# Softmax sums from columns of ones beside V, and scores in 64x64 tiles, in a cross-attention and expert kernel

## The chip, the cores and the metric

The kernel runs on one core of a Trainium2 chip. The metric is device time in microseconds (us) of one execution. A core has TensorE (PE, matmuls; its weight loads are listed as PEld), VectorE (DVE), ScalarE (ACT), GpSimd (POOL) and SyncE (SP, which here only issues DMAs). Each engine works through its own instruction list in order and waits on semaphores.

## The reference, cut to what matters

All data is float32. There are 64 batches of 64 query rows of 256 values, and 64 context rows of 128 values for each batch. The first part is a residual cross-attention with 16 heads of 16 values:

```
xn   = layernorm(x)                              # 64 x 64 x 256
q    = head_norm(xn @ Wq + bq)                   # per head of 16 values
main = the first 48 context rows, dca = the last 16
k, v = head_norm(main @ Wk..), main @ Wv..       # bk, bv beside
kd, vd from dca with their own weights
ctx  = softmax(q k^T / 4) v  +  softmax(q kd^T / 4) vd   # two softmaxes, 48 and 16 keys
x    = x + ctx @ Wo + bo
```

The second part is a residual feed-forward with a shared expert and 16 routed experts, two for each row. The change doesn't touch it, but for where some small buffers of its router lie.

## The kernel before, in words

The 64 batches are 32 pairs (128 query rows fill the 128 partitions), and two pairs (u = 0, 1) are one group, so there are 16 groups. The attention is a software pipeline over groups, written by hand: `main_loop` calls each engine's `step(i)` for i from -1 to 17, of which i = 3 to 12 is a hardware loop. In one step(i) each engine works on several groups: x of i+3 is loaded, x, q, k and v of i+2 are projected, q and k of i+1 are normalised and laid out, softmax and the product with V belong to i, the output projection and the residual to i-1, the second layer norm to i-2. The order of the calls in `step` is the order on that engine, and an instruction that waits holds up all behind it.

- VectorE: `inverse_roots` (L1361) makes all inverse square roots of a step in a chain of ten small instructions, the first of them L353; the maxima and subtractions of the scores of u = 0 stand between them. Then `residual` (L1460), `spread_roots` (L1421), `inverse_sums` of u = 0 (L1451: two sums and one reciprocal), maxima and subtractions of u = 1, `residual_stats`, `copy_qkv` (L1406), `inverse_sums` of u = 1, `x_stats`, `head_vars`. L1343 is the last instruction of either layer norm's statistics, on 128x2 values.
- GpSimd: `normalise_k` and `normalise_q` (L637, L646), which writes q twice, once for each batch of the pair, with zeros for the rows of the other batch; `normalise_probs` (L670), `add_bo` (L631), `dca_blocks` (L658).
- TensorE: `transpose_y`, `attn_out(i-1)` (L1098), `scores(i, 1)` (L1050), transposes of x, k and xn2, `project_q`, `transpose_q` of u = 0, `project_kv`, `transpose_q` of u = 1, `transpose_probs(i, 0)`, `route`, `probs_v(i, 0)` (L1077), `scores(i+1, 0)`, `transpose_probs(i, 1)`, `probs_v(i, 1)`.
- ScalarE: copies between PSUM and SBUF, exponentials, the two normalisations of x, squares, and `mask_v` (L800), which masks the V rows to block form.
- SyncE: `replicate_v` (L478) copies V rows and the stored DCA rows to both halves of the partitions (8 DMAs a step), then the loads of y and x and the stores of xn2.

Scores: one transposed q of 128 rows holds two heads' values and both batches by zeros; four matmuls of 128x128 by 256 columns fill `score_ps`. The probabilities are divided by their sums on GpSimd before they are transposed; `probs_v` multiplies with block V into a transposed context directly, which ScalarE copies for the output projection.

Of the kernel before, what the change touches and what calls it, by code (L numbers as in the profile page):

```python
# [25 lines left out]
P = 128  # L26
NB, SQ, D = 64, 64, 256
SK, KD = 64, 128
DCA = 16
# [12 lines left out]
CW = 4 * SK  # L42
HP = H // 2
TT = PAIRS // 2
SLOT_TILES = 48
N_CONST = 12
# [41 lines left out]
def xattn_moe(nc, x, ctx, Wq, bq, Wk, bk, Wv, bv, Wkvd, bkvd, qn_w, qn_b, kn_w, kn_b, kd_w, kd_b, Wo, bo,  # L88
              router, e_bias, w_up, w_down, sh_up, sh_down, out):
    stack = ExitStack()  # L90
    with stack:
# [3 lines left out]
        def sem(name):  # L95
            return stack.enter_context(nc.semaphore(name))

        bank = [stack.enter_context(nc.psum_tensor(f"bank{i}", [P, 512], F32)) for i in range(4, 8)]
# [3 lines left out]
               [b[:, :] for b in bank]  # L102


        vd_dram = nc.dram_tensor("vd_dram", [PAIRS * DCA, 2 * D], F32, kind="Internal").ap()
        vd_blocks = vd_dram.rearrange("(u t k) n -> t u k n", u=8, k=DCA)
# [9 lines left out]
        half = sb("half", [P, 2])  # L116
        slotm = sb("slotm", [P, 2])
# [6 lines left out]
        bkv_sb = sb("bkv_sb", [P, 2 * D])  # L124
# [7 lines left out]
        q_bias2 = sb("q_bias2", [P, 2])  # L132
# [13 lines left out]
        sel = sb("sel", [P, PAIRS, E])  # L146
        pair_sums = sb("pair_sums", [P, TT * NG, 6])
        gsum = sb("gsum", [P, TT, NG])
        gtmp = sb("gtmp", [P, TT, NG])
        goh = sb("goh", [P, 2, TT, NG])  # L150
        oh = sb("oh", [P, 2, PAIRS, E])
        etmp = sb("etmp", [P, PAIRS, E])
        tile_cnt = sb("tile_cnt", [P, PAIRS, E])
# [7 lines left out]
        past = sb("past", [1, SLOT_TILES, E])  # L161
# [5 lines left out]
        desc = sb("desc", [P, 1, E])  # L167

# [11 lines left out]
        kv_sb = sbl("kv_sb", [P, 2, 2 * D])  # L180
        sq = sbl("sq", [P, 2, 2, D])
        qn = sbl("qn", [P, 2, 2 * D])
# [4 lines left out]
        q_rstd2 = sbl("q_rstd2", [P, 2, H, 2])  # L187
        qT = sbl("qT", [P, 2, SETS, P])
        k_bd = sbl("k_bd", [P, 2, SETS, 4, SK])
        v_rep = sbl("v_rep", [P, 2, 2 * D])  # L190
        v_bd = sbl("v_bd", [P, 2, 2 * D])
        probs = sbl("probs", [P, 2, H, SK])
        pmax = sbl("pmax", [P, 2, 2, H])
        psum_ = sbl("psum_", [P, 2, 2, H])
        prec = sbl("prec", [P, 2, 2, H])
# [14 lines left out]
        kv_d = XN2[:, 0:4 * DT, :].rearrange("p (n c) d -> p n (c d)", c=2)  # L210
        sq_d = XN2[:, 4 * DT:6 * DT, :]
        kn_d = XN2[:, 6 * DT:8 * DT, :].rearrange("p (t c) d -> p t (c d)", c=2)
# [45 lines left out]
        s_sum = sem("softmax_sums")  # L258
# [11 lines left out]
        s_rstd = sem("head_rstd_ready")  # L270
# [7 lines left out]
        s_v = sem("v_replicated")  # L278
        s_vbd = sem("v_blocks_ready")
# [60 lines left out]

        x_rows = x.rearrange("b s d -> (b s) d")
        out_rows = out.rearrange("b s d -> (b s) d")

        def row1(v):
            return v.rearrange("(a n) -> a n", a=1)

# [1410 lines left out]
```

## Time and profile before

| | us |
|---|---|
| median of 3 runs | 643.29 |
| lowest to highest | 641.64 to 643.62 |
| span of the profiled execution | 644.6 |
| VectorE busy | 453.7 (70%) |
| TensorE busy | 525.5 (82%) |
| ScalarE busy | 348.8 (54%) |
| GpSimd busy | 288.1 (45%) |

The profile gives one execution's span, from its first to its last instruction, and no time around it. The attention takes from some 43 us to 383 us, the routing and the experts follow. Busy times overlap between engines; whoever wants to know what sets the time must ask which engine waits for which, in each stage.

### The profile page before, as it was taken

The page shows a single profiled execution, that of the slowest core. Times are in us where ns is not written, and L with a number is a line of the kernel's source. Part 1 is how long each engine was busy: PE and PEld are TensorE (multiplying, and loading weights), DVE is VectorE, ACT ScalarE, POOL GpSimd, SP SyncE. Part 2 cuts the span into 40 slices and gives each one's busy share as a digit, 9 for nine tenths or more (in the row PEclk, how much of TensorE's full clock was granted, in tenths as well). Part 3 has the DMA queues.
Part 4 walks back from the last instruction along what each step waited for, and adds up shares of the span by engine and source line. Part 5 has one row for each costly group of instructions (what it writes and reads, how often), then busy time and mean ns, then how long its engine had stood idle before and what let it go on. Part 6 is the DMA issues. An engine that isn't in the chain of part 4 may idle for free.

```text
span 644.6 us, 12343 instructions
## 1 busy us (share of the span) xinstructions
PE 525.5 (82%) x3539; PEld 410.0 (64%) x3540; DVE 453.7 (70%) x1114; ACT 348.8 (54%) x663; POOL 288.1 (45%) x358
## 2 busy tenths in 40 slices
PE   4457879878797788887898688994799998879977
PEld 2234657666575666766676555764799987865746
DVE  2966899999999998989987858985144446741343
ACT  1235668666786667857677426140566665506240
POOL 2012565534655346443465200577772057605760
PEclk9778998899999989979898879999699999879989
DMA  5251233243432434323333311953799788838343
GB/s 146 90 126 49 74 105 107 70 129 110 132 108 67 130 108 132 97 78 122 112 115 115 131 66 51 344 184 105 232 329 317 230 276 261 279 115 263 114 135 108
DMA packets 83052, 94.50 MB, mean 147 GB/s; under 512 B 8000, under 2 KB 72272, under 8 KB 83024
## 3 DMA queue, kind: packets, MB, share of 16 engines
q1 hardware_dynamic: 72976, 72.14, 36.0%
q0 software_dynamic: 6144, 16.79, 8.0%
q10 hardware_dynamic: 3904, 5.24, 2.7%
q8 instruction: 13, 0.21, 0.1%
q14 instruction: 15, 0.12, 0.1%
HBM read 40.66 MB, written 42.99 MB: 130 GB/s over the span
## 4 chain that ended last, share of the span: by engine, by line
PE 27%; POOL 24%; issue 22%; DVE 14%; DMA 4%; ACT 2%; DVEq 1%; POOLq 0%; ACTq 0%; SPq 0%
POOL slot_x L704 5%; PE bank L1276 4%; POOL probs L673 4%; POOL kdT L721 4%; PE score_ps L1264 4%; POOL XN L721 3%; PE bank L1185 3%; POOL qn L652 3%; PE probsT_ps L1251 2%; PE probsT_ps L1103 2%; PE bank L1017 2%; PE score_ps L1026 2%; POOL k_bd L665 2%; POOL kn L641 2%; DVE psum_ L1454 2%
## 5 line engine op out<-in xcount | busy, mean ns | idle before, releaser
L673 POOL TENSOR_TENSOR probs<-probs,prec 128x768 f32<-128x768 f32 x64 | 65.7, 1046 | 53.6 <-DVE prec L1458 53.6
L704 POOL DMA_INDIRECT slot_x<-XN,slot_i x64 | 62.3, 973 | 55.4 <-DVE slot_i L1610 36.2
L641 POOL TENSOR_TENSOR kn<-kv_sb,rst 96x512 f32<-96x512 f32 x16 | 16.9, 1054 | 136.4 <-DVE q_rstd L1425 136.4
L1060 PE MATMUL score_ps<-k_bd,qT 128*128 128x256 f32 x256 | 66.9, 407 | 4.7 <-DVE probs L1446 3.6
L740 ACT ACTIVATE probsT<-probsT_ps 128x1024 f32<-128x1024 f32 x32 | 32.8, 1024 | 55.6 <-PE probsT_ps L1073 55.6
L1185 PE MATMUL bank<-sd_sb,hid 128*128 128x256 f32 x256 | 58.8, 392 | 3.5 <-DVE res L1728 3.5
L1060 PEld LDWEIGHTS score_ps<-k_bd,qT 128*128 128x128 f32 x256 | 50.7, 203 | 13.7 <-issue 5.2
L1185 PEld LDWEIGHTS bank<-sd_sb,hid 128*128 128x128 f32 x256 | 50.6, 198 | 12.5 <-issue 5.2
L1276 PE MATMUL bank<-down_sb,ea 128*128 x192 | 49.3, 404 | 8.2 <-DVE ea L1662 8.2
L1073 PE MATMUL probsT_ps<-ident,probs 128*128 128x128 f32 x256 | 35.3, 282 | 21.6 <-POOL probs L673 21.6
L1669 DVE COPY ey<-bank 128x512 f32<-128x512 f32 x48 | 30.9, 684 | 23.1 <-PE bank L1276 23.1
L1073 PEld LDWEIGHTS probsT_ps<-ident,probs 128*128 128x128 f32 x256 | 29.1, 144 | 28.2 <-POOL probs L673 27.9
L1092 PE MATMUL bank<-probsT,v_bd 128*32 128x64 f32 x1024 | 25.2, 243 | 26.6 <-ACT probsT L740 26.5
L1264 PEld LDWEIGHTS score_ps<-XN,tile_w 128*128 128x128 f32 x384 | 46.1, 197 | 0.8 <-issue 0.2
L1264 PE MATMUL score_ps<-XN,tile_w 128*128 128x128 f32 x384 | 46.3, 280 | 0.0
L1276 PEld LDWEIGHTS bank<-down_sb,ea 128*128 128x128 f32 x192 | 37.2, 204 | 13.6 <-issue 8.8
L1436 DVE TENSOR_REDUCE pmax<-score_ps 128x16 f32<-128x768 f32 x64 | 41.7, 672 | 5.1 <-PE score_ps L1060 5.0
L1446 DVE TENSOR_TENSOR probs<-score_ps,pmax 128x768 f32<-128x768 f32 x64 | 42.3, 682 | 0.0
L740 ACT ACTIVATE XN<-probsT_ps 128x512 f32<-128x512 f32 x48 | 26.0, 595 | 28.6 <-PE probsT_ps L1251 28.6
L1454 DVE TENSOR_REDUCE psum_<-probs 128x16 f32<-128x768 f32 x64 | 40.6, 673 | 0.5 <-ACT probs L812 0.3
L1092 PEld LDWEIGHTS bank<-probsT,v_bd 128*32 128x32 f32 x1024 | 20.3, 121 | 31.4 <-issue 31.3
L1103 PE MATMUL probsT_ps<-wo_sb,ctxT 128*128 128x256 f32 x128 | 40.0, 468 | 0.0
(210 smaller groups left out, 1210.9 us busy)
## 6 DMA issues: line engine op xcount, KB each, us to landing
slot_x<-zeros SPq DMA_DIRECT2D x32, 384.0 KB, 3.4
XN<-slot_x SPq DMA_DIRECT2D x24, 512.0 KB
slot_y<-ey SPq DMA_DIRECT2D x24, 512.0 KB, 3.9
v_rep<-kv_sb SPq DMA_DIRECT2D x64, 96.0 KB, 2.3
x_in<-in_x SPq DMA_DIRECT2D x16, 256.0 KB, 2.7
XN<-xn SPq DMA_DIRECT2D x16, 256.0 KB, 2.8
xn2T_dram<-xn2T SPq DMA_DIRECT2D x32, 128.0 KB, 2.3
xT_ch<-xn2T_dram SPq DMA_DIRECT2D x8, 512.0 KB, 4.8
```

Source lines behind the costliest of these rows:

```text
L673: last = pool.tensor_tensor(probs[:, u, :, lo:hi], probs[:, u, :, lo:hi], prec[:, u, c, :].unsqueeze(2).to_broadcast([P, H, hi - lo]), ALU ...
L704: pool.indirect_dma_start(slot_x[f][:, :], bass.IndirectOffsetOnAxis(ap=slot_i[:, k, t:t + 1], axis=0), XN2[:, t, :], None).then_inc(s_sca ...
L721: pool.indirect_dma_start(gath[b][:, h, k, j, :], None, slot_y[f][:, :], bass.IndirectOffsetOnAxis(ap=gidx[:, b, h, k, j:j + 1], axis=0))\
L740: return act.activation(dst, src, ACT.Copy)
L1060: last = pe.matmul(score_ps[:, s * CW:(s + 1) * CW], qT[:, u, s, :], k_bd[:, u, s, :, :].rearrange("p j k -> p (j k)"), start=True, stop=True)
L1073: last = pe.transpose(probsT_ps[:, n // 4, (n % 4) * P:(n % 4 + 1) * P], flat[:, n * P:(n + 1) * P], ident[:, :])
L1092: last = pe.matmul(ctx_ps[u][32 * n:32 * n + 32, col:col + 64], v_bd[:, u, b * D + (4 * c + n) * 32:b * D + (4 * c + n) * 32 + 32], probsT ...
L1103: last = pe.matmul(bank[2 + u][:, 0:D], ctxT[:, u, k, :], wo_sb[:, k, :], start=(k == 0), stop=(k == KC - 1))
L1185: last = pe.matmul(o, hid[:, j, m, t * P:(t + 1) * P], sd_sb[:, m, :], start=(m == 0), stop=(m == NM - 1))
L1264: last = pe.matmul(bank[h][:, j * P:(j + 1) * P], tile_w[:, h, j, k * MI:(k + 1) * MI], xtT[:, h, j, k, :], start=(k == 0), stop=(k == KC ...
L1276: last = pe.matmul(bank[4 + 2 * h + j // 2][:, (j % 2) * D:(j % 2 + 1) * D], ea[:, h, j * P:(j + 1) * P], down_w[:, bass.ds(offs[j], D)], ...
L1454: dve.tensor_reduce(psum_[:, u, c, :], probs[:, u, :, lo:hi], AX.X, ALU.add).then_inc(s_sum, 1)
```

## The change

- The product with V is turned round: the transposed probabilities are the stationary operand and V the moving one. For each pair of heads V stands in a row of 68 columns: 34 for the main keys (32 values, a 1, a 0), 34 for the DCA keys (with 0 and 1). So one product gives, for each head pair, the two softmaxes' unnormalised contexts and their sums. VectorE takes the reciprocals of the sums and multiplies the product (`normalise_ctx`), GpSimd adds the main and DCA parts (`add_ctx`), TensorE transposes the context (`transpose_ctx`), ScalarE copies it (`copy_ctx`), then comes the output projection, now after `transpose_q` and ahead of `project_kv`.
- The sums on VectorE and the products on GpSimd (`normalise_probs`) go, as does `spread_roots`.
- q is no longer doubled; the scores are eight matmuls of 64 rows by 64 columns of the array.
- V is written by VectorE with its padding, and SyncE places rows of 1088 values (`place_v`, double-buffered); ScalarE's `mask_v` goes.
- The residual of both pairs is one instruction and stands behind the subtractions of u = 1, ahead of `copy_qkv`.
- The hardware loop's body holds two steps.

```diff
+PVW = 2 * (2 * HD + 2)
+VROW = H // 2 * PVW
-            with eng.Fori(3, GROUPS - 3) as i:
-                step(i)
+            with eng.Fori(0, (GROUPS - 6) // 2) as m:
+                step(2 * m + 3, 1)
+                step(2 * m + 4, 0)
...
# setup: bias loads
-            sp.dma_start(bkv_sb[:, 0:D], all_rows(bk)).then_inc(s_w, 16)
-            sp.dma_start(bkv_sb[:, D:], all_rows(bv)).then_inc(s_w, 16)
+            for c, v in enumerate((bk, bv)):
+                key, value = (v.rearrange("(h t d) -> t h d", t=2, d=HD)[t] for t in range(2))
+                sp.dma_start(heads_of(bk_sb[:, :])[:, c * HP:(c + 1) * HP, :], all_rows(key)).then_inc(s_w, 16)
+                for b in range(2):
+                    sp.dma_start(heads_of(bv_sb[:, b, :])[:, c * HP:(c + 1) * HP, :], all_rows(value)).then_inc(s_w, 16)
...
# SyncE
+            def place_v(g, par):
                 wait_alone(sp, s_kv, g + 1)
-                if since(g, 1):
-                    sp.wait_ge(s_vbd, g)
-                for c in range(2):
+                if since(g, 2):
+                    sp.wait_ge(s_pv_ps, 2 * g - 2)
+                for q in range(2):
                     for u in range(2):
+                        sp.dma_start(v_aug[64 * q:64 * q + SM, par, u, :], v_pad_rows[u * SM:(u + 1) * SM, q, :])\
+                            .then_inc(s_v, 16)
+                        sp.dma_start(v_aug[64 * q + SM:64 * q + SK, par, u, :],
+                                     vd_dram[q][bass.ds(2 * DCA * g + DCA * u, DCA), :]).then_inc(s_v, 16)
...
# GpSimd
             def normalise_q(g):
-                pool.wait_ge(s_rstd, g + 1)
+                pool.wait_ge(s_root, N_ROOT * (g + 2))
+                    pool.wait_ge(s_qT_ps, g)
+                pool.tensor_tensor(qn[:, :, :].rearrange("p u (h d) -> p (u h) d", d=HD),
+                                   q_sb[:, :, :].rearrange("p u (h d) -> p (u h) d", d=HD),
+                                   rst[:, 1, 32:64].unsqueeze(2).to_broadcast([P, 32, HD]), ALU.mult)\
+                    .then_inc(s_qn, 1)
+            def add_ctx(g, u):
+                pool.wait_ge(s_norm, 2 * g + (u + 1))
+                if since(g, 1):
+                    pool.wait_ge(s_c_ps, g)
+                pool.tensor_tensor(ctx_sb[:, u, :].rearrange("p (h d) -> p h d", d=HD), ctx_parts[:, u, :, 0, :],
+                                   ctx_parts[:, u, :, 1, :], ALU.add).then_inc(s_ctx, 1)
-            def normalise_probs(g, u):
...
# GpSimd's step
                 if active(i + 1):
                     normalise_k(i + 1)
                     normalise_q(i + 1)
-                if active(i):
-                    normalise_probs(i, 0)
+                if active(i - 1):
+                    add_ctx(i - 1, 1)
                 if active(i + 2):
                     add_bo(i + 2)
                 if active(i + 1):
                     dca_blocks(i + 1)
                 if active(i):
-                    normalise_probs(i, 1)
+                    add_ctx(i, 0)
...
# TensorE
             def scores(g, u):
+                for c in range(KC):
+                    for r in range(2):
+                        for b in range(2):
+                            last = pe.matmul(score_ps[64 * b:64 * b + 64, r * 512 + c * CW:r * 512 + (c + 1) * CW],
+                                             qT[64 * r:64 * r + 64, u, c, 64 * b:64 * b + 64],
+                                             k_bd[64 * r:64 * r + 64, u, 2 * b + c, :, :].rearrange("p j k -> p (j k)"),
+                                             start=True, stop=True)
...
+                for r in range(2):
+                    for c in range(KC):
+                        for j in range(2):
+                            n, hp = 2 * c + j, 2 * r + j
+                            for b in range(2):
+                                last = pe.matmul(pv_ps[u][64 * b:64 * b + 64, c, hp * PVW:(hp + 1) * PVW],
+                                                 probsT[:, u, r, n * P + 64 * b:n * P + 64 * b + 64],
+                                                 v_aug[:, par, u, b * VROW + (4 * c + hp) * PVW:
+                                                       b * VROW + (4 * c + hp + 1) * PVW],
+                                                 start=True, stop=True)
+                last.then_inc(s_pv_ps, 1)
...
# TensorE's step
                 if active(i + 2):
                     transpose_y(i + 2)
-                if active(i - 1):
-                    attn_out(i - 1)
                 if active(i):
                     scores(i, 1)
                 if active(i + 2):
                     transpose_x(i + 2)
                 if active(i + 1):
                     transpose_k(i + 1)
+                if active(i - 1):
+                    transpose_ctx(i - 1)
                 if active(i - 2):
                     transpose_xn2(i - 2)
                 if active(i + 2):
                     project_q(i + 2)
                 if active(i + 1):
-                    transpose_q(i + 1, 0)
+                    transpose_q(i + 1)
+                if active(i - 1):
+                    attn_out(i - 1)
                 if active(i + 2):
                     project_kv(i + 2)
...
# VectorE
+            def normalise_ctx(g, u):
+                dve.wait_ge(s_pv_ps, 2 * g + (u + 1))
+                if since(g, 1):
+                    dve.wait_ge(s_ctx, 2 * g + (u - 1))
+                blocks = pv_ps[u].rearrange("p c (h e) -> p c h e", e=PVW // 2)
+                dve.reciprocal(prec[:, u, :, :].rearrange("p (c h) t -> p c h t", c=KC), blocks[:, :, :, 2 * HD:])\
+                    .then_inc(s_rsum, 1)
+                dve.wait_ge(s_rsum, 2 * g + (u + 1))
+                dve.tensor_tensor(ctx_parts[:, u, :, :, :].rearrange("p (c h) t d -> p c h t d", c=KC),
+                                  blocks[:, :, :, 0:2 * HD].rearrange("p c h (t d) -> p c h t d", t=2),
+                                  prec[:, u, :, :].rearrange("p (c h) t -> p c h t", c=KC).unsqueeze(4)
+                                  .to_broadcast([P, KC, HP, 2, HD]), ALU.mult).then_inc(s_norm, 1)
             def residual(g):
                 dve.wait_ge(s_xbo, g + 1)
+                dve.wait_ge(s_o_ps, g + 1)
+                rows = X2[:, bass.ds(2 * g, 2), :]
+                dve.tensor_tensor(rows, bank[3].rearrange("p (u n) -> p u n", u=2), rows, ALU.add).then_inc(s_x2, 1)
...
# VectorE's step
                 inverse_roots(i)
                 if active(i - 1):
-                    residual(i - 1)
-                if active(i + 1):
-                    spread_roots(i + 1)
+                    normalise_ctx(i - 1, 1)
                 if active(i):
-                    inverse_sums(i, 0)
                     for c in range(2):
                         score_max(i, 1, c)
                     for c in range(2):
                         subtract_max(i, 1, c)
                 if active(i - 1):
+                    residual(i - 1)
                     residual_stats(i - 1)
                 if active(i + 2):
                     copy_qkv(i + 2)
                 if active(i):
-                    inverse_sums(i, 1)
+                    normalise_ctx(i, 0)
```

## Rows read from the trace of the kernel before

**Rows 1.** Busy time by window, settled loop: window; length; engines with instructions; clock; DMA.

```profile
126.00:226.00 100.00, 79.65 (x731) 62.47 (x730) 92.00 (x225) 72.06 (x131) 48.87 (x61) 1.00 0.35 110
```

**Rows 2.** Timeline of VectorE: start, length, first root of two steps.

```profile
76.53 0.20 DVE L353 TENSOR_SCALAR rst<-rst 128x68 int32<-128x68 int32 x1
...
337.08 0.54 DVE L353 TENSOR_SCALAR rst<-rst 128x68 int32<-128x68 int32 x1
```

**Rows 3.** Timeline of VectorE, one settled step.

```profile
176.44 0.20 DVE L353 TENSOR_SCALAR rst<-rst 128x68 int32<-128x68 int32 x1 [0.77 <-DVE rst L1358]
...
181.17 0.76 DVE L1465 TENSOR_TENSOR X<-probsT_ps,X 128x256 f32 x2
...
181.97 1.27 DVE L1454 TENSOR_REDUCE psum_<-probs 128x16 f32<-128x768 f32 x2
183.35 0.35 DVE L1458 RECIPROCAL prec<-psum_ 128x32 f32<-128x32 f32 x1
183.62 1.22 DVE L1436 TENSOR_REDUCE pmax<-score_ps 128x16 f32<-128x768 f32 x2
...
185.95 0.74 DVE L1338 BATCH_NORM_STATS2 bn<-X 128x6 f32 x2
...
187.13 2.17 DVE L1343 TENSOR_SCALAR rst<-mv 128x2 f32<-128x2 f32 x1
189.21 0.68 DVE L1410 TENSOR_TENSOR q_sb<-bank,bq_sb 128x512 f32<-128x512 f32 x1
189.81 1.27 DVE L1417 TENSOR_TENSOR kv_sb<-score_ps,bkv_sb 96x512 f32<-96x512 f32 x2
...
192.64 0.69 DVE L1338 BATCH_NORM_STATS2 bn<-x_in 128x6 f32<-128x256 f32 x2
...
193.76 0.53 DVE L1343 TENSOR_SCALAR rst<-mv 128x2 f32<-128x2 f32 x1
194.21 0.67 DVE L1353 TENSOR_REDUCE stat<-sq 128x32 f32<-128x512 f32 x1
```

**Rows 4.** Timeline of GpSimd, the same step.

```profile
182.21 1.05 POOL L641 TENSOR_TENSOR kn<-kv_sb,rst 96x512 f32<-96x512 f32 x1 [7.40 <-DVE q_rstd L1425]
183.23 2.07 POOL L652 TENSOR_TENSOR qn<-q_sb,q_rstd 128x512 f32<-128x512 f32 x2
...
187.27 1.28 POOL L634 TENSOR_TENSOR X<-x_in,bo_sb 128x512 f32 x1
```

**Rows 5.** Timeline of TensorE, the same step.

```profile
177.16 0.69 PE L1092 MATMUL bank<-probsT,v_bd 128*32 128x64 f32 x32 [1.20 <-ACT probsT L740]
...
178.10 1.92 PE L1103 MATMUL probsT_ps<-wo_sb,ctxT 128*128 128x256 f32 x8
...
182.44 0.66 PE L1008 MATMUL bank<-ident,xn 128*128 128x128 f32 x4 [0.69 <-ACT xn L759]
...
184.22 1.95 PE L1017 MATMUL bank<-wq_sb,xnT 128*128 128x256 f32 x8
...
186.45 1.88 PE L1026 MATMUL score_ps<-wkv_sb,yT 128*96 128x512 f32 x4
...
188.60 1.04 PE L1073 MATMUL probsT_ps<-ident,probs 128*128 128x128 f32 x8
```

**Rows 6.** Timeline of ScalarE, the copy behind those transposes.

```profile
189.67 1.02 ACT L740 ACTIVATE probsT<-probsT_ps 128x1024 f32<-128x1024 f32 x1 [0.48 <-PE probsT_ps L1073]
```

**Rows 7.** Busy time by window around a fall of the clock.

```profile
233.20:236.60 3.40, 1.42 (x10) 0.86 (x8) 2.41 (x8) 0.50 (x1) 1.72 (x2) 1.00 0.49 168
236.60:240.00 3.40, 2.73 (x37) 2.34 (x38) 3.33 (x11) 2.08 (x5) 0.00 (x0) 0.50 0.00 0
```

**Rows 8.** Timeline of the setup, all engines.

```profile
1.43 0.95 POOL L605 MEMSET kv_sb<- 128x1024 f32 x1
...
8.40 0.43 SPq L458 DMA_DIRECT2D bkv_sb<-in_L_xattn_bk  x1
...
13.25 0.74 DVE L1317 TENSOR_REDUCE wmean<-wq_sb 128x16 f32<-128x256 f32 x2 [6.33 <-DMA bkv_sb<-in_L_xattn_bv]
```

More of the change, by code:

```diff
@@ L96, in sem @@
             return stack.enter_context(nc.semaphore(name))
-        bank = [stack.enter_context(nc.psum_tensor(f"bank{i}", [P, 512], F32)) for i in range(4, 8)]
+        bank_ps = stack.enter_context(nc.psum_tensor("bank", [P, 4, 512], F32))
         score_ps = stack.enter_context(nc.psum_tensor("score_ps", [P, 2 * 512], F32))
@@ L679, in _, with step @@
             pool.wait_ge(s_const, N_CONST)
-            def step(i):
+            def step(i, par):
                 if active(i + 1):
@@ L1004, in transpose_x @@
                 pe.wait_ge(s_xn, g + 1)
+                if since(g, 3):
+                    pe.wait_ge(s_norm, 2 * g - 4)
                 for u in range(2):
@@ L1025, in project_kv @@
                 for b in range(2):
-                    last = pe.matmul(kv_ps[b][0:MR, :], yT[:, b, 0:MR], wkv_sb[:, :], start=True, stop=True)
+                    for c in range(2):
+                        last = pe.matmul(bank[c][0:MR, b * D:(b + 1) * D], yT[:, b, 0:MR], wkv_heads[:, c, :, :],
+                                         start=True, stop=True)
                 last.then_inc(s_kv_ps, 1)
@@ L1055, in scores @@
                 if u == 0 and active(g + 1):
[L1056 removed]
+                    wait_alone(pe, s_kv, g + 2)
                 else:
[L1058 to L1061 removed]
+                    wait_alone(pe, s_sub, 2 * g + u)
+                for c in range(KC):
[5 more added lines that the diff above has]
+                                             start=True, stop=True)
                 last.then_inc(s_s_ps, 1)
             def transpose_probs(g, u):
[L1065 removed]
+                pe.wait_ge(s_exp, 2 * g + (u + 1))
                 if u == 1:
@@ L1096, in probs_v, with transpose_ctx @@
+            def transpose_ctx(g):
+                pe.wait_ge(s_ctx, 2 * g + 2)
+                for u in range(2):
+                    for c in range(KC):
+                        last = pe.transpose(bank[2][:, (u * KC + c) * P:(u * KC + c + 1) * P],
+                                            ctx_sb[:, u, c * P:(c + 1) * P], ident[:, :])
                 last.then_inc(s_c_ps, 1)
             def attn_out(g):
+                pe.wait_ge(s_c, g + 1)
                 for u in range(2):
-                    pe.wait_ge(s_c, 2 * g + (u + 1))
@@ L1208, in _ @@
                     pe.wait_ge(s_xT, 1)
-                for s in range(SETS):
-                    last = pe.transpose(dca_bank[t][:, s * P:(s + 1) * P], kn_d[:, t, s * P:(s + 1) * P], ident[:, :])
+                for b in range(2):
+                    for c in range(KC):
+                        last = pe.transpose(dca_bank[t][:, (b * KC + c) * P:(b * KC + c + 1) * P],
+                                            kn_d[:, t, b, c * P:(c + 1) * P], ident[:, :])
                 last.then_inc(d_kT_ps, 1)
```

347 lines of the change are left out of this document (154 added, 193 removed).

## The prediction

> **What bounds the kernel now.** I read the busy table by stage first: in the settled attention loop VectorE is busy 92.00 of 100 us, TensorE 80, and the granted clock is 1.00, its 2.4 GHz level [rows 1]. Then VectorE's timeline for the length of a step: the first inverse-root instruction of a step stands at 76.53 and, thirteen steps later, at 337.08, so 20.04 us a step [rows 2]. The reader is to see in one step [rows 3] that VectorE is nearly never idle, but that 2.17 us of it is one instruction on 128x2 values, which takes 0.53 or 2.17 us although it has two values a partition: both times GpSimd is at work, on the X row and the block products behind it the longer time [rows 4]. Then TensorE's and ScalarE's timelines [rows 5, 6], for who must deliver when: the projections end at 188.3 and VectorE copies them at 189.2, so that order is close to binding already, although VectorE looks like the bound.
>
> **What VectorE gains by instructions.** Per step two pairs of sum reductions go (2 x 1.27), and the root spreading (about 0.1): -2.6. Two products of 128x512 from PSUM come: +1.2, each at the 0.60 pitch of the query copy. The two reciprocals stay. The two residual adds become one, -0.1. GpSimd loses the four probability products and one of two query products and gains two 128x256 additions, so it is idle at both places where the tiny instruction now waits: at least 0.16 of each is its own (2.17 - 2.0, 0.53 - 0.35): -2.0 and -0.35. All in all -3.85, which would be 16.2 us a step if VectorE bounded it.
>
> **But the order changes what it waits for.** I walk one step of the changed kernel, in us after its first inverse-root instruction, at today's durations. A TensorE group hands over 0.16 before its busy time ends [rows 5].
> - Roots with the first scores' maxima between them: 4.5, as now [rows 3]. The normalised x reaches TensorE at 6.0, as now [rows 5].
> - VectorE: reciprocal and product for the previous group's second half, 4.7 to 5.8. GpSimd: keys 1.05 and now one query product 1.04, from 4.7 to 6.75, and only behind them the addition, 0.6 (half of a query product; 0.4 to 0.65 by the X row's 1.28 for 512), to 7.4 [rows 4].
> - TensorE: four transposes of the context 0.44 (half of the eight at 188.60) to 7.85, xn2 to 8.3, query projection 1.79 to 10.1, query transposes to 10.5, output projection 1.76 to 12.3 [rows 5]. Today that output projection runs at 1.7 to 3.4, in time in which TensorE would wait for x anyway; the move puts it, with the context transposes, between x and the key/value projection.
> - VectorE has been free since 8.2 (maxima and subtraction of the second scores, 183.62 to 185.95, 2.3). In its order stands the residual, which needs the output projection: it waits from 8.2 to 12.4. Behind the residual are queued its statistics and the copies of q, k and v, for which project_q has long been ready. Residual 0.6 to 13.0, statistics 1.3 to 14.3, three copies 1.8 to 16.1.
> - TensorE meanwhile: key/value projection 1.72 to 14.0, probability transposes 0.88 to 14.9, ScalarE's copy 1.02 [rows 6] to 16.1, probabilities times V about 1.0 to 17.2.
> - VectorE waits for that from 16.1 to 17.2; then reciprocal and product 1.0, x statistics 1.2 (192.64 to 194.21 less the port wait), head variances 1.5, loop registers 0.4 (the 0.77 of idle ahead of the step's first row, in full only on every second step now that the loop body holds two): 21.3.
> So with the clock at 2.4 GHz a step is 21.3 instead of 20.04: +1.26 x 13 = +16.4.
>
> **Unknown costs of the tiled matmuls.** No row has a matmul on 64 rows. Today's 16 products of 128x32 tiles with V take 0.69 where one after the other they would take 16 x 64/512 of the 0.86 that a 128x512 projection takes (1.88 for two), 1.7: column tiles overlap [rows 5]. Scores: eight matmuls of 256 columns, 0.43 each by the output projection's row: 0.85 if four tiles overlap, 1.7 if only the column tiles do, 3.4 if none. I take 1.0, the side on which the V row lies. Probabilities times V: 16 x 68 columns, 0.9 with two overlapping, 1.8 with none; I take 1.0. TensorEngine Tiling (Array Packing) of the Trainium skill, Key Properties, has tiles load and multiply in parallel; by it 0.85 and 0.9 would stand, which moves the sum by 0.1 a step.
>
> **The clock.** Faster scores leave TensorE idler at the wrong place: from 0.4 to 6.0 it has about 1.0 us of scores to do, the rest is waiting for the subtraction and for x. Today TensorE was busy 1.42 us between 233.2 and 236.6, and from 236.6 on the clock stood at 0.50 [rows 7]; that happens now and then, because its gaps today are split by the output projection. In the changed order such a gap is in every step, and what follows it is the chain above, from 6.0 to 14.9, nearly all TensorE. Half speed at 1.2 GHz over 1.5 to 3 us worth of that work costs as much again. I take 2.1 in four steps of five: 1.7 a step, x 13 = +22; bounds 0 and 3.0 x 13 = 39. TensorE: Matmul & The Clock Gate in the Trainium skill, HAM oscillation, says that idle gaps throttle the engine again so that the next burst starts cold; by that rule the gap of each step is paid in each step, the trace agrees for the one gap in rows 7.
>
> **Ends and setup.** In the last three steps little else covers the context's way through VectorE (1.0), GpSimd (0.6), TensorE (0.44) and ScalarE: +1 each, +3 (0 to 6). Setup: the bias loads become six of 64-byte pieces instead of two, four more issues of about 0.45 in front of the wait that ends at 13.25 (+2, 1 to 5) [rows 8]; the eight first adds of V and K (0.60 each) become three smaller ones, about 0.75 together: +1. GpSimd's zeroing of 10,950 values a partition at 951 ns per 1024 is 10 us, over by 14, before VectorE needs it at 18 [rows 8]. Sixteen stores instead of eight to DRAM end before the second group's V is placed. Setup +3 (0 to 7). Placed V rows are 590 KB more a step in a queue with DMA share 0.35 [rows 1], needed over 10 us later: 0. After the loop nothing moves.
>
> **Sum.** 644.6 + 16.4 + 22 + 3 + 3 = 689. The profile gives its span only, with nothing around it; the median of the runs is 1.3 below it: **687.7**, call it 687.
>
> **Rivals.**
> - VectorE binds after all (faster). If residual and copies find their inputs at 8.2, the step falls to 16.2: -3.85 x 13 = -50, with setup 595. Its place is the wait in front of the residual; it decides for faster wherever the output projection ends before 11.1 in the step. For it: 92% busy. Against: project_q cannot begin before 7.8 and 4 us of TensorE stand between it and the residual. A part of it (5 to 50 us) counts here. Chance 0.08.
> - The clock stays up, the order alone costs: 644.6 + 22.4 - 1.3 = 666. For it: if row tiles do not overlap, scores of 1.7 keep TensorE busy in the gap. Chance 0.27.
> - VectorE's shift is caught by GpSimd's key product. Today the root spreading holds GpSimd back; now it starts on the last root, as the second shift (two SBUF inputs) does, 0.1 after it. If GpSimd is first, shift and all behind it stand for 1.05 to 2.1: +1.9 x 13 more, 712. The row that it rests on: 2.17 while GpSimd ran [rows 3, 4]. Chance 0.14. SBUF — State Buffer of the Trainium skill, section SBUF: two separate sides, has that port pair as a lock held for a whole instruction; by it the 1.05 is the least that a lost race costs.
> - No change within 0.3% (+-2 us): 0.02.
>
> **How the numbers follow.** The likeliest (0.49) is 687, its own range 676 to 698 by the clock's bounds. For 8 in 10 the range reaches down below the warm case, 652, and up to the lost race, 714. What can be told from no change here is about 0.3%. Faster 0.08, same 0.02, slower 0.90.
>
> **What would show it.** Right: VectorE idle 3 to 5 us before the residual, released by the output projection; the reductions gone and VectorE's busy share down to about 65 to 70%; clock rows at 0.50 in most steps; the 128x2 instruction always under 0.6; steps of 22 to 24. Wrong: steps under 20, a residual that waits for nothing, or shifts of over 1 us (the third rival).

## The result and the profile after

| | before | changed |
|---|---|---|
| median, us | 643.45 (4 runs) | 720.56 (4 runs, 716.04 to 721.06) |
| span of the profiled execution | 644.6 | 718.5 |
| mean granted clock | 0.919 | 0.861 |
| VectorE busy | 453.7 (70%) | 418.2 (58%) |

The changed kernel is slower, 1.118 times the time of the one before, 95% interval 1.114 to 1.122. VectorE has 35 us less to do, and the kernel takes 77 us longer. The forecast had the direction and the two mechanisms of the loop, and the time lies 6.6 us above its range of 652 to 714.

First the timeline of VectorE for where the spans part: start, length, instruction. These are the first inverse roots of step -1, of step 1 and of step 14.

```profile
63.17 0.20 DVE L374 TENSOR_SCALAR rst<-rst 128x68 int32<-128x68 int32 x1
...
98.91 0.20 DVE L374 TENSOR_SCALAR rst<-rst 128x68 int32<-128x68 int32 x1
...
407.24 0.20 DVE L374 TENSOR_SCALAR rst<-rst 128x68 int32<-128x68 int32 x1
```

Before, the last two stood at 76.53 and 337.08 [rows 2] and the first at 42.73. So of the 73.9 us that the span grew, 20.4 are in the setup, 1.9 in steps -1 and 0, 47.8 in thirteen steps (23.72 us each in place of 20.04) and 6.1 in the last ones; what follows the loop gave 2.3 back. The window over the thirteen steps (length; busy PE, PEld, DVE, ACT, POOL; then the granted clock):

```profile
98.91:407.24 308.33, 228.41 (x2136) 188.43 (x2131) 201.80 (x527) 157.49 (x256) 80.44 (x117) 0.83 0.41 115
```

**One settled step.** VectorE, with the idle time ahead of an instruction and what ended it in brackets; it answers to [rows 3].

```profile
242.03 0.20 DVE L374 TENSOR_SCALAR rst<-rst 128x68 int32<-128x68 int32 x1 [0.86 <-DVE rst L1386]
...
246.55 0.23 DVE L1431 SCALAR_TENSOR_TENSOR shift<-mv,rst 128x2 f32<-128x2 f32 x2
246.73 0.36 DVE L1481 RECIPROCAL prec<-bank 128x32 f32<-128x32 f32 x1
247.12 0.69 DVE L1484 TENSOR_TENSOR ctx_parts<-bank,prec 128x512 f32<-128x512 f32 x1
...
248.93 1.27 DVE L1470 TENSOR_TENSOR probs<-score_ps,pmax 128x768 f32<-128x768 f32 x2
256.28 0.69 DVE L1493 TENSOR_TENSOR X<-probsT_ps,X 128x512 f32 x1 [6.08 <-PE probsT_ps L1134]
...
258.43 0.17 DVE L1371 TENSOR_SCALAR rst<-mv 128x2 f32<-128x2 f32 x1
258.51 0.69 DVE L1439 TENSOR_TENSOR q_sb<-bank,bq_sb 128x512 f32<-128x512 f32 x1
...
261.18 0.36 DVE L1481 RECIPROCAL prec<-bank 128x32 f32<-128x32 f32 x1 [0.79 <-PE bank L1113]
```

The residual (L1493) waits 6.08 us for the output projection, and the copy of q behind it finds its matmul long done. The 2.17 us of the tiny instruction (L1343, now L1371) have gone. TensorE in the same step, against [rows 5]:

```profile
245.21 1.90 PE L1075 MATMUL score_ps<-k_bd,qT 64*64 64x256 f32 x16 [3.03 <-DVE probs L1470]
248.12 1.11 PE L1020 MATMUL bank<-ident,xn 128*128 128x128 f32 x4 [1.00 <-ACT xn L788]
...
251.37 2.53 PE L1029 MATMUL bank<-wq_sb,xnT 128*128 128x256 f32 x8
...
254.17 1.89 PE L1134 MATMUL probsT_ps<-wo_sb,ctxT 128*128 128x256 f32 x8
```

It idles 3.03 us ahead of the scores and another 1.00 ahead of x, and then does the work for which VectorE stands. (The trace lists two records for a float32 matmul that isn't a transpose: the x16 are the eight products of the scores.) The windows of that step (length; busy PE, PEld, DVE, ACT, POOL; then the granted clock) show at what speed; they answer to [rows 7].

```profile
242.03:245.80 3.77, 0.74 (x12) 0.52 (x14) 3.67 (x12) 0.70 (x1) 0.00 (x0) 1.00 0.59 156
245.80:252.60 6.80, 5.80 (x33) 4.56 (x26) 4.26 (x11) 4.75 (x10) 5.43 (x8) 0.50 0.51 113
252.60:265.30 12.70, 10.88 (x125) 9.12 (x125) 7.20 (x20) 6.83 (x11) 0.74 (x1) 1.00 0.32 112
```

After a stretch with 0.74 us of matmuls in 3.77 the clock is at 1.2 GHz for 6.80 us, of which TensorE is busy 5.80; each of the thirteen steps has such a stretch.

**The setup.** All engines, against [rows 8].

```profile
3.02 3.73 POOL L643 MEMSET v_aug<- 128x4352 f32 x1
...
5.88 6.47 DVE L1349 TENSOR_SCALAR wmean<-wmean 128x32 f32<-128x32 f32 x1
...
8.93 3.06 SPq L478 DMA_DIRECT2D bv_sb<-in_L_xattn_bk  x2
...
14.18 3.84 SPq L478 DMA_DIRECT2D bv_sb<-in_L_xattn_bv  x2
...
22.51 0.74 DVE L1347 TENSOR_REDUCE wmean<-wq_sb 128x16 f32<-128x256 f32 x2 [9.37 <-DMA bv_sb<-in_L_xattn_bv]
...
28.59 9.48 SPq L494 DMA_DIRECT2D vd_dram<-v_aug  x8
...
38.11 10.62 SPq L494 DMA_DIRECT2D vd_dram<-X  x8
...
57.44 0.39 SPq L457 DMA_DIRECT2D x_in<-in_x  x1
...
60.31 0.75 DVE L1366 BATCH_NORM_STATS2 bn<-x_in 128x6 f32<-128x256 f32 x2 [11.46 <-DMA x_in<-in_x]
```

Two waits of VectorE make it. The centring of the weights starts at 22.51 in place of 13.25 and waits for the last bias load: the first of six loads in 64-byte pieces is issued in 0.44 us, the other five hold the queue for 1.5 to 2.1 us each, where an ordinary one takes 0.43. And the second group's x is loaded only at 57.44, because SyncE issues it behind sixteen stores of V rows and the wait for them: the stores take 20.1 us to issue and the wait another 7.8 (before, 5.3 and 3.5 for eight stores).

### The profile page after: what moved, and what is told of

Its sections match the earlier page's. It is cut to its first block, busy times and chain, and to the rows that moved or that the text cites. A ratio compares the mean times of both kernels' runs of the same rounds, so it can differ in the third digit from the quotient of the medians.

```text
span 718.5 us, 12718 instructions
## 1 busy us (share of the span) xinstructions
PE 535.1 (74%) x3859; PEld 426.4 (59%) x3860; DVE 418.2 (58%) x1063; ACT 313.6 (44%) x567; POOL 239.2 (33%) x316
## 4 chain that ended last, share of the span: by engine, by line
PE 36%; DVE 21%; issue 16%; POOL 12%; DMA 6%; SPq 4%; ACT 3%; DVEq 1%; ACTq 0%; POOLq 0%
PE bank L1029 5%; POOL slot_x L733 4%; PE probsT_ps L1134 4%; PE bank L1309 4%; PE score_ps L1039 3%; PE score_ps L1297 3%; POOL kdT L750 3%; POOL XN L750 3%; PE bank L1113 3%; PE bank L1216 2%; PE bank L1020 2%; PE probsT_ps L1284 2%; PE probsT_ps L1090 2%; ACT probsT L769 2%; SPq L494 2%
## 5 line engine op out<-in xcount | busy, mean ns | idle before, releaser
L691 POOL TENSOR_TENSOR ctx_sb<-ctx_parts 128x256 f32<-128x256 f32 x32 | 23.5, 735 | 177.0 <-DVE ctx_parts L1484 176.0
L1075 PE MATMUL score_ps<-k_bd,qT 64*64 64x256 f32 x512 | 43.2, 452 | 41.1 <-DVE probs L1470 39.6
L769 ACT ACTIVATE probsT<-probsT_ps 128x1024 f32<-128x1024 f32 x32 | 32.8, 1024 | 78.6 <-PE probsT_ps L1090 78.6
L1493 DVE TENSOR_TENSOR X<-probsT_ps,X 128x512 f32 (+1 forms) x16 | 11.1, 692 | 93.1 <-PE probsT_ps L1134 93.1
L671 POOL TENSOR_TENSOR kn<-k_sb,rst 96x512 f32<-96x512 f32 x16 | 16.9, 1055 | 138.7 <-DVE rst L383 138.7
L828 ACT ACTIVATE probs<-probs 128x1024 f32<-128x1024 f32 x32 | 34.1, 1065 | 63.8 <-DVE probs L1470 63.8
L1113 PE MATMUL bank<-v_aug,probsT 128*64 128x68 f32 x1024 | 38.3, 228 | 30.3 <-ACT probsT L769 28.4
L1113 PEld LDWEIGHTS bank<-v_aug,probsT 128*64 128x64 f32 x1024 | 34.6, 140 | 35.0 <-issue 35.0
L1075 PEld LDWEIGHTS score_ps<-k_bd,qT 64*64 64x64 f32 x512 | 21.0, 149 | 49.3 <-issue 45.1
L1020 PE MATMUL bank<-ident,xn 128*128 128x128 f32 x64 | 17.8, 433 | 37.4 <-ACT xn L788 37.4
L1029 PE MATMUL bank<-wq_sb,xnT 128*128 128x256 f32 x128 | 43.6, 501 | 1.1 <-ACT xnT L769 0.8
L1020 PEld LDWEIGHTS bank<-ident,xn 128*128 128x128 f32 x64 | 11.4, 216 | 48.0 <-DVE ctx_parts L1484 23.8
```

Source lines behind the costliest of these rows:

```text
L769: return act.activation(dst, src, ACT.Copy)
L1020: last = pe.transpose(bank[6][:, (u * KC + k) * P:(u * KC + k + 1) * P], xn[:, u, k * P:(k + 1) * P], ident[:, :])
L1029: last = pe.matmul(bank[5][:, u * D:(u + 1) * D], xnT[:, u, k, :], wq_sb[:, k, :], start=(k == 0), stop=(k == KC - 1))
L1075: last = pe.matmul(score_ps[64 * b:64 * b + 64, r * 512 + c * CW:r * 512 + (c + 1) * CW], qT[64 * r:64 * r + 64, u, c, 64 * b:64 * b + 64] ...
L1113: last = pe.matmul(pv_ps[u][64 * b:64 * b + 64, c, hp * PVW:(hp + 1) * PVW], probsT[:, u, r, n * P + 64 * b:n * P + 64 * b + 64], v_aug[:, ...
```

## The experiments

All are the changed kernel with the edit given. Before's median was 644.4, 644.5 and 644.9 us beside e1 to e4, e5 to e8, and e9 and e10, and 694.0 beside e11 and e12, which ran on another chip. "Step" is the mean of the same thirteen steps.

| kernel | median, us | ratio to before, 95% | step, us |
|---|---|---|---|
| changed | 720.56 | 1.114 to 1.122 | 23.72 |
| e1 bias loads whole | 712.58 | 1.098 to 1.109 | 23.73 |
| e2 x load on another queue | 717.05 | 1.106 to 1.117 | 23.76 |
| e3 TensorE's gaps filled | 692.87 | 1.067 to 1.079 | 21.87 |
| e4 projection a step later | 690.30 | 1.065 to 1.075 | 21.72 |
| e5 x statistics into the wait | 703.80 | 1.082 to 1.100 | 22.53 |
| e6, e10 order rewritten | 662.70, 664.02 | 1.019 to 1.036, 1.023 to 1.036 | 19.99, 19.97 |
| e7 order rewritten, projection a step later | 629.29 | 0.963 to 0.982 | 17.19 |
| e8 as e7, with e1 and e2 | 613.66 | 0.945 to 0.962 | 17.00 |
| e9 as e8, loads still earlier | 613.27 | 0.945 to 0.954 | 17.23 |
| e11 key product behind the shifts | 768.64 | 1.105 to 1.115 | 23.69 |
| e12 as e8, with e11 | 658.25 | 0.946 to 0.954 | 16.83 |

**e1.**

```diff
-                key, value = (v.rearrange("(h t d) -> t h d", t=2, d=HD)[t] for t in range(2))
-                sp.dma_start(heads_of(bk_sb[:, :])[:, c * HP:(c + 1) * HP, :], all_rows(key)).then_inc(s_w, 16)
-                ...
+                sp.dma_start(b_in[:, c * D:(c + 1) * D], all_rows(v)).then_inc(s_w, 16)
```

> The changed kernel with one edit: bk and bv are loaded whole (two loads of 128 rows by 1 KB in place of six whose rows are cut into 64-byte pieces) and VectorE sorts them into bk_sb and the two halves of bv_sb with three copies, before the weights are centred. Theory A (the 64-byte pieces hold the setup back): the centring that started at 22.5 us starts at about 13.5 us, three copies add about 1 us, everything behind it moves up, the stores of the V rows too, and the first inverse root of step -1 moves from 63.2 to about 55 us; the time is about 712 us (709 to 715). Rival B (the centring also waits for the other weight loads, or the queue is bound by its number of loads and not by their pieces): the root moves by less than 3 us and the time stays within 718 to 721 us. The steps keep their 23.7 us in both.

The copies started at 13.28 and the reductions at 14.01 in place of 22.51, the first root of step -1 came at 54.56 in place of 63.17, and the median is 8.0 us lower. Theory A: the pieces cost 8.6 us of the setup more than the three copies do. From e1's timeline:

```profile
14.01 0.74 DVE L1345 TENSOR_REDUCE wmean<-wq_sb 128x16 f32<-128x256 f32 x2
```

**e2.**

```diff
-            load_y(1)
-            load_x(1)
+            act.wait_ge(s_xbo, 1)
+            act.dma_start(x_in[:, :, :], ...).then_inc(s_x, 16)      # on ScalarE, with y's, ahead of squares(0)
```

> The changed kernel with one edit: the loads of the second group's context and x rows are issued from ScalarE's queue before the squares of group 0, and no longer from SyncE's queue behind the sixteen stores of V rows and the wait for them. Theory A (these loads queue behind the wait, nothing else holds them): the statistics of x that started at 60.3 us start at 51 to 53 us, the first inverse root of step -1 comes at about 54 to 56 us in place of 63.2 us, and the time is about 713 us (710 to 716). Rival B (the DMA engines are full with the stores until about 56 us and the loads land only then, whichever queue issues them): the root moves by 2 us at most, time 718 to 721 us. Rival C (the root moves, but GpSimd's addition to x, which still waits for the stores, hands the wait on to the key blocks and the first scores): the first steps lose what the setup gained, time 717 to 721 us although the root is early.

Between A and B, with a little of C: the root stands at 58.52, 4.65 us earlier, and the first root of step 1 at 95.86, 3.05 us earlier. The median is 3.5 us lower (its interval overlaps that of the changed kernel; the root carries the finding). The row, VectorE's timeline of e2:

```profile
55.66 0.75 DVE L1371 BATCH_NORM_STATS2 bn<-x_in 128x6 f32<-128x256 f32 x2 [6.42 <-DMA x_in<-in_x]
```

The load was issued at 50.49, where ScalarE's own order let it, and took 5.1 us to land among the stores; the other loads of x take 2.7 (median). Both things held it: the queue, and the traffic.

**e3.** In every step, three matmuls that nobody reads, two of them ahead of the transposes of the context rows y:

```diff
+                    for _ in range(2):     # in transpose_y, ahead of its transposes
+                        pe.matmul(bank[5], ident[:, :], wo_sb[:, :, :].rearrange("p k n -> p (k n)"), ...)
+            def fill_b():                  # behind scores(i, 1): one into bank[7]
```

> The changed kernel with idle time of TensorE filled by matmuls whose results nobody reads: two of 128x512 columns ahead of the context transposes and one after the second half's scores, in every step (about 0.87 us each at the full clock). Theory C (a good part of the 23.7 us step is TensorE at the half clock in its critical stretches): the granted clock stays at 1.00 in the loop, the step falls to 21.3 to 21.8 us and the time to about 692 us (685 to 698). Rival O (the order of the work sets the step, and the work that ran at the half clock is not on the chain): the mean clock rises all the same and the step falls by less than 0.5 us, time 713 to 720 us. Rival F (the fillers stand in the chain themselves and cost more than the clock gives): the step gets longer, 24 us or more, time above 724 us.

Theory C. The window over its thirteen steps has the clock at its upper level throughout, and in one of its steps the residual still waits, while TensorE stands idle behind either filler, ahead of the scores and ahead of x (so rival F falls; it is the same in all thirteen):

```profile
98.57:382.89 284.32, 231.22 (x2214) 173.59 (x2209) 201.82 (x527) 154.20 (x256) 80.37 (x117) 1.00 0.44 125
```

```profile
255.09 1.09 PE L1084 MATMUL score_ps<-k_bd,qT 64*64 64x256 f32 x16 [0.72 <-DVE probs L1482]
...
258.88 0.65 PE L1025 MATMUL bank<-ident,xn 128*128 128x128 f32 x4 [1.64 <-ACT xn L789]
...
264.94 0.69 DVE L1505 TENSOR_TENSOR X<-probsT_ps,X 128x512 f32 x1 [3.93 <-PE probsT_ps L1143]
```

So the 47.8 us divide: 308.3 - 284.3 = 24.0 by the clock, and 284.3 - 260.6 = 23.8 that stay at the full clock. (The kernel before is taken as it is, with a few slow stretches of its own: its granted clock in those steps is 0.95.) This run also bears on what TensorE: Matmul & The Clock Gate of the Trainium skill says in HAM oscillation, that idle gaps bring the slow clock back: with the gaps filled no window fell.

**e4.**

```diff
-                if active(i - 1):
-                    attn_out(i - 1)            # behind transpose_q
+                if active(i - 2):
+                    attn_out(i - 2)            # behind transpose_y, at the step's start
-                    residual(i - 1)            # behind the second half's subtractions
+                    residual(i - 2)            # ahead of them; second layernorm and router follow at i - 3
```

> The changed kernel with the output projection of a group and its residual moved to the start of the next step (all that follows them, the second layernorm and the router, one step later too, so that there is one more step at the end), which is where the kernel before had the place for them; no operation is added or taken away. Theory O (VectorE stands 6 us in every step before the residual, because the projection now ends behind its place in the order): the wait ahead of the residual falls below 1 us, the step falls from 23.7 to about 21.1 us, the added last step costs about 5 us, and the time is about 690 us (683 to 700). Rival C (the clock and the matmuls set the step, and VectorE only waits at another place for the same TensorE work): the step stays at 23.3 to 23.9 us, and the time is 720 to 728 us with the added step.

Theory O. VectorE's timeline of e4 has the residual without any wait, and what stood behind it now waits by itself:

```profile
254.58 0.68 DVE L1502 TENSOR_TENSOR X<-probsT_ps,X 128x512 f32 x1
...
260.00 0.69 DVE L1446 TENSOR_TENSOR q_sb<-bank,bq_sb 128x512 f32<-128x512 f32 x1 [1.09 <-PE bank L1031]
262.17 0.69 DVE L1453 TENSOR_TENSOR k_sb<-score_ps,bk_sb 96x512 f32<-96x512 f32 x1 [1.47 <-PE score_ps L1041]
...
265.52 0.36 DVE L1490 RECIPROCAL prec<-bank 128x32 f32<-128x32 f32 x1 [2.07 <-PE bank L1117]
```

The steps are 2.0 us shorter and not 2.6, and stay above the 20.04 of the kernel before: smaller waits, for q, for k and for the product with V, took up the rest.

**e5.** `x_stats(i + 3)` moved ahead of `residual(i - 1)`, nothing else.

> The changed kernel with one move in VectorE's order: the statistics of the x rows three groups ahead (two bn_stats, two bn_aggr and one scalar, 1.5 us, which wait for nothing late) stand ahead of the residual and no longer at the end of the step. Theory O (VectorE stands 6 us ahead of the residual, and all that it does behind the residual is on the chain that sets the step): the 1.5 us go into the wait, the wait falls to about 4.6 us, the step falls by 1.5 to 1.9 us, and the time is about 697 us (691 to 702). Rival C (TensorE and its clock set the step; VectorE's own work is hidden behind it): the same 1.5 us only turn up as idle time before another matmul's result, step down by less than 0.4 us, time 714 to 722 us.

Theory O in direction (16.8 us less), but short of its size. The waits of VectorE between 180 and 340 us (waited for: us, times, longest):

```profile
DVE bn L1369 <- DMA x_in<-in_x: 21.5, 7, 3.4
DVE X L1498 <- PE probsT_ps L1136: 12.8, 7, 2.8
```

The moved statistics do wait for something late, the x load, 3.1 us a step.

**e6 and e10.** The calls in a step, in their order on TensorE and VectorE (ScalarE and GpSimd were reordered too). e6 leaves out a wait, so that it transposes scores where it should transpose their exponentials, and its time alone would prove nothing; e10 has the wait again:

```
TensorE: scores(1), y, xn2, ctx, x, k transposed, attn_out, project_q, transpose_probs(0), project_kv,
         probs_v(0), transpose_q, route, scores(0) of i+1, transpose_probs(1), probs_v(1)
VectorE: roots, normalise_ctx(1), max/subtract(1), residual, its statistics, copy q, x_stats, copy kv,
         normalise_ctx(0), head_vars
```

> The changed kernel with the same operations and the same distance in steps between a group's parts, but another order within the step on the four engines (residual ahead of copies as before, x statistics between the copy of the queries and that of keys and values, projection of keys and values behind the first transposes of the probabilities, squares and logits later). Theory O (waits at the seams between engines, made by an order fitted to the old durations, are the loss; the operations themselves are cheaper): the step falls from 23.7 to 18.4 to 19.5 us, below the 20.04 us of the kernel before, and the time is about 655 us (648 to 668). Rival C (the changed operations themselves, the clock above all, cost the time): the step stays above 21.5 us and the time above 690 us.

> The order of e6 with one correction: in e6 ScalarE took the exponent of the second half ahead of that of the first, so that the transposes of the first half, which count exponents, no longer waited for their own and took scores without it; here the first half's exponent stands ahead again, where the rest of the order is that of e6. Theory O: as in e6, a step of 19.5 to 21 us (19.8 and 21.1 us in turn there) and a time of about 662 us (655 to 670). Rival W (e6 was short because the first half's transposes didn't wait): the wait returns on the way from the first half's scores to its context, the step is 21.5 us or more, the time above 680 us.

Both 19.97 to 19.99 us a step, medians 1.3 us apart: rival W falls, the missing wait gave nothing. Theory O: the rewritten order, with the same operations and the same distances, takes 3.75 us out of a step, though it ends a little above the 18.4 to 19.5 that e6 expected. A part of that can have come through the clock, which is at 0.94 in e10's thirteen steps against 0.83; against e3's step of 21.87 at the full clock e10's is still 1.9 us shorter.

**e7.** e4's shift with the calls in this order:

```
TensorE: y, attn_out of i-2, scores(1), x, k, xn2, ctx transposed, project_q, transpose_probs(0), project_kv,
         probs_v(0), transpose_q, transpose_probs(1), scores(0) of i+1, route, probs_v(1)
VectorE: roots, normalise_ctx(1), residual of i-2, max/subtract(1), its statistics, copy q, x_stats, copy kv,
         normalise_ctx(0), head_vars
```

> As e4 (projection and residual at the start of the next step), with the order within the step rewritten as well so that each engine meets its inputs when they are there. Theory O: VectorE becomes the engine that sets the step; its operations in one step sum to 16.2 us, so the step is 16.7 to 17.7 us, VectorE's busy share in the loop is above 90%, the granted clock stays at 1.00 there, and with one more short step at the end the time is about 628 us (618 to 642), faster than the kernel before. Rival C (the clock and TensorE set the step): TensorE's 16 to 17 us of matmuls at the full clock would allow this too, but at the half clock in parts the step stays above 19.5 us and the time above 662 us.

Theory O, in each number. The window over the thirteen steps of e7:

```profile
97.60:321.04 223.44, 196.31 (x2126) 157.70 (x2122) 200.62 (x520) 154.45 (x251) 80.60 (x117) 0.98 0.55 157
```

VectorE is busy 200.62 of 223.44 us, 90%, 15.4 us a step; before it was 92% at 18.4 us a step [rows 1]. The saving in VectorE's work is real, and it arrives once VectorE is again the engine that sets the step. (e7's whole time, 0.963 to 0.982 of before's, still carries the setup of the changed kernel.)

**e8, e9.**

> e7 with both edits of the setup (the biases loaded whole and sorted on the core; the second group's loads from ScalarE's queue). In the old order these gave 8.6 and 4.7 us at the first inverse root of step -1. Theory A (they add up, since the one moves the start of the stores and the other takes the loads out from behind their end): 13 us less than e7, about 615 us (604 to 629). Rival S (with the shorter steps the placing of the first V rows, which waits for all sixteen stores, becomes the wait of the first step): only the 8.6 us of the biases arrive, 3 to 5 us less gain, about 619 us.

15.6 us less than e7, and the root of step -1 comes 13.2 us earlier: theory A. With e9 it is the best of both kernels and all variants, 0.953 times before.

> e8 with its two loads from ScalarE's queue issued right behind the copy of the first transposed x rows (at about 32.5 us) and no longer behind the copies of the transposed keys (at 41 us). Theory A (in e8 VectorE stands 6.7 us ahead of the x statistics because the load, issued at 42.4 us among the stores, lands at 47.8 us): the load now lands at about 39 us, the statistics run right behind the copies of keys and values at 41 us, the first inverse root of step -1 waits for the squares alone and comes at 45 to 46 us in place of 50.7 us, and the time is about 608 us (604 to 612). Rival S (the placing of the first V rows, behind all sixteen stores that end at about 46.5 us, is late instead): the root is early, the first two steps give most of it back, time 611 to 615 us.

Rival S in effect. The root came at 44.33, 6.4 us earlier, and step -1 then took 19.9 us in place of 15.3. From e9's timeline:

```profile
49.35 0.63 SPq L503 DMA_DIRECT2D v_aug<-v_pad  x1
...
56.42 0.40 SPq L458 DMA_DIRECT2D x_in<-in_x  x1
...
59.36 0.75 DVE L1383 BATCH_NORM_STATS2 bn<-x_in 128x6 f32<-128x256 f32 x2 [4.78 <-DMA x_in<-in_x]
```

The next x load stands in SyncE's queue behind the placing of V, and that behind the stores; in e8 it was issued at 55.70. The stores' end is the fixed point.

**e11, e12.**

```diff
             def normalise_k(g):
                 pool.wait_ge(s_root, N_ROOT * (g + 2))
+                pool.wait_ge(s_shift, g + 2)
```

> The changed kernel with one wait more: GpSimd's key product waits for VectorE's two shifts as well as for the last inverse root. In its profile the pair of shifts (128x2 values) takes 0.23 us in one step and 1.19 us in the next, seven times of thirteen the long one, with GpSimd's key product (1.05 us) running beside it. Theory P (the key product, released by the same root, is at times ahead of the second shift and holds it for its own length; x, the first product of the context and the residual stand behind it): no pair over 0.3 us any more, GpSimd starts 0.1 to 0.3 us later, the long steps shorten by 0.7 to 0.95 us and the time falls by 4 to 7 us, to about 715 us (712 to 718). Rival N (the step's end is set by TensorE's chain behind x and the addition on GpSimd, which now start later): the pair is short in every step, and the time stays at 719 to 723 us.

> e8 with the same wait. In e8's loop VectorE is busy nine tenths of the time, and six of its pairs of shifts take 1.11 us or more. Theory P: each of these gives back about 0.9 us, since VectorE sets the step, and GpSimd has time to spare there: steps of 16.8 us at most, time about 608 us (605 to 611). Rival N (VectorE only meets the next wait earlier, since GpSimd's products and so the transposes of keys, queries and context start 0.2 us later): time 612 to 615 us.

On that chip before takes some 49 us more, and the excess lies behind the loop: what follows the last root takes 306.8 us in e11 and 310.1 in e12, against 261.6 in the changed kernel and 266.1 in e8. So the loop's rows are compared. The ratio of e11, 1.110, is no gain: 49 us more on both sides would make 1.111 of the changed kernel's 1.118.

e11: no pair is long any more, but the steps are 24.2 and 23.6 in turn where they were 24.6 and 23.3, 23.69 on average: rival N. (What still alternates is the idle time ahead of the first root, 0.85 and 0.32 us.) Here is the residual of a step with a long pair, in the changed kernel, and of its like in e11:

```profile
280.30 0.69 DVE L1493 TENSOR_TENSOR X<-probsT_ps,X 128x512 f32 x1 [5.92 <-PE probsT_ps L1134]
...
280.54 0.69 DVE L1494 TENSOR_TENSOR X<-probsT_ps,X 128x512 f32 x1 [6.54 <-PE probsT_ps L1135]
```

From the step's first root it is 15.0 us in the one and 14.7 in the other, so of the 0.96 us that the pair gave back, 0.6 went into this wait. The clock can have had a part in that: in e11 it is at 0.79 over the thirteen steps, in the changed kernel at 0.83. Whether the edit or the chip lowered it is open, and so is what the edit would bring at an equal clock.

e12: where VectorE sets the step, the loop from the first root of step -1 to the last root took 291.1 us against 295.2 in e8, and the thirteen steps 218.8 against 221.0. Four settled steps, two of which had a long pair, took 67.8 against 68.5, so a long pair costs about 0.34 us there. That is theory P in direction, with less than half of its 0.9; the whole time doesn't tell e12 from e8.

## Why the prediction was off

- **Setup, +3 (0 to 7): the step that failed.** It was +20.4. Two prices were wrong. The four more bias loads were counted at 0.45 us of queue each, from ordinary loads, +2 in all; in 64-byte pieces they take up to 2.1 us to issue, and the wait grew by 9.3 (e1: 8.6). And "sixteen stores end before the second group's V is placed" asked only who needs the stores: the second x load stands behind the wait for them in SyncE's order, so that VectorE waited 11.46 us for it. From the centring to the root it is 40.7 us in place of 29.5. e2 and e9 took 4.65 and, by e8's root, 6.4 us out of that at the root. With +20.4 in place of +3 the sum is 705, inside the range.
- **Order, +16.4: right in mechanism, too small.** In e3, with the clock up, the wait ahead of the residual is 4.1 us on average of the thirteen steps, where 4.2 was forecast. The walk put the residual at 12.4; e3 has it at 12.7 in a step with a short pair of shifts and at 13.0 (264.94 - 251.92) in one with a long pair, of which the thirteen steps hold seven. They cost 23.8 us, since the walk's step of 21.3 was 21.87. By those two rows the long pair makes up 0.2 of this 0.57 a step; the rest lies in small differences along the walk that no run takes apart.
- **Clock, +22: right.** 24.0 by e3, a slow stretch in every step.
- **VectorE's work, -3.85 a step: too large.** It was busy 238.5 us in the thirteen steps before and 201.8 after, -2.8 a step. The long pair of shifts, +0.5 a step, is a part of the difference. The sum doesn't use the term, only the first rival does. The busy share came as forecast, 65% (201.8 of 308.3 us) for 65 to 70%, and the tiny instruction of the statistics is always short.
- **Tiled matmuls, 1.0 each:** 1.09 and 1.17 of busy time at the full clock, and less the 0.16 at a group's end that the walk takes off, 0.9 and 1.0. The copies of q, k and v behind the residual and the wait for the product with V came about as walked: 0.79 ahead of the reciprocal, 1.1 forecast.
- **Last steps +3, measured +6.1;** steps -1 and 0, +1.9, were not in the sum. Together: 17.4 of setup, 9.4 of loop, 3.1 and 1.9, less 2.3 after the loop, are the 29.5 between the sum and the span of 718.5.
- **VectorE binds (0.08):** the rival named the right lever. e4 made its condition true, the residual waits for nothing, and that alone brought the step only to 21.7, for other waits took its place. With the order rewritten as well (e7) the step fell to 17.2, a full 1 us above the rival's 16.2.
- **GpSimd catches the shift (0.14):** it happens, in every second step in the settled loop and at the small price (0.96 us a time); taking it away left the mean step as it was in e11, at a lower clock. SBUF — State Buffer of the Trainium skill, SBUF: two separate sides, gives the port pair to whichever starts first, a VectorE instruction with two SBUF inputs or a GpSimd one that reads SBUF, for its whole length; the pair of 1.19 us beside a key product of 1.05 agrees.

## What to carry to other kernels

Here the work taken off the busiest engine was worth nothing until its inputs came earlier too. So walk the new order by due times, and rewrite it with the change: the same operations took 23.7 us a step in one order, 20.0 in another, and 17.2 with the output projection a step later as well. Filling a matmul engine's gap with unread work is a cheap test that separates a slow clock from a late input. In a setup, ask for each new DMA what stands behind it in its queue, and how many pieces it is cut into.

## What the runs showed of the hardware

- A load of 128 rows in 64-byte pieces (1024 of them) behind another such holds its queue for 1.5 to 2.1 us; whole rows of 1 KB take 0.43.
- A VectorE instruction on 128x32 values stood for 6.47 us while GpSimd zeroed three buffers (3.73, 3.73 and 1.97 us): it began during the first and ended with the third. In e8 it stood for 4.59 us and got through behind the second. An instruction that waits through one of GpSimd's need not be the next.
- Eight float32 matmuls on 64x64 tiles with 256 columns take 1.09 us at the full clock, sixteen on 128x64 tiles with 68 columns 1.17 (16 and 32 records in the trace).
- The shift pair is long exactly in every second settled step, with the loop's two-step body; what in the two halves decides the race was not tried.
- A load of x of 256 KB, issued from ScalarE's queue while the stores run, takes 5.1 us to land in e2 and 8.3 in e9, against a median of 2.7 for the others.
